# Attention with 32-bit probabilities and values in one product per block, and heads folded by 32-bit products

## The reference

```python
qkv = (xf @ qkv_w.T).reshape(B, H, W, 3, h, d)        # 16 heads of 8 channels
for a in range(KSZ):                                   # 7 x 7 neighbours
    for c in range(KSZ):
        l = einsum('bhijd,bhijd->bhij', q, kac) + bias
        logits.append(l)
attn = softmax(stack(logits), axis=-1)
out = sum over the 49 neighbours t of attn[..., t, None] * vac
y = out @ proj_w.T + proj_b
```

## Time and profile before

| what | value |
|---|---|
| median of 3 runs | 3155.05 us (3146.11 to 3156.77) |
| profiled execution | 3149.2 us |
| its span, first to last instruction | 3147.4 us |
| mean granted TensorE clock | 0.904 of full speed |
| PE busy | 2482.8 us, 79% of the span |
| PEld busy | 2108.7 us, 67% |
| DVE busy | 2353.8 us, 75% |
| ACT busy | 2122.5 us, 67% |
| POOL busy | 2360.1 us, 75% |

### The profile page before, as it was taken

The page is one execution under the profiler, slowest core; times in us unless marked ns, Lnnn a source line. Parts: engine busy times, 40 slices in busy tenths (PEclk is TensorE's granted clock), DMA queues, the critical chain, the costliest instruction groups (busy, mean ns, idle before and its releaser), DMA issues. The chain is left out here.

```text
span 3147.4 us, 119476 instructions
## 1 busy us (share of the span) xinstructions
PE 2482.8 (79%) x34587; PEld 2108.7 (67%) x34692; DVE 2353.8 (75%) x12579; ACT 2122.5 (67%) x5724; POOL 2360.1 (75%) x2808
## 2 busy tenths in 40 slices
PE   4788887888788878888888878888709999999633
PEld 2677777777777777777777777777606666666522
DVE  2688887888788878888788878888746666666444
ACT  0677777777677777777777777777726777777400
POOL 2578888888888888888888888888946777777600
PEclk9999999999899999999999989999959999999855
DMA  2566555555555655555565555556455444444499
GB/s 49 145 126 119 121 124 119 114 122 118 112 106 122 123 118 110 118 117 117 114 120 118 118 109 119 121 117 123 92 99 94 93 92 93 93 93 92 98 314 299
DMA packets 743654, 378.47 MB, mean 120 GB/s; under 512 B 414595, under 2 KB 712227, under 8 KB 743078
## 3 DMA queue, kind: packets, MB, share of 16 engines
q1 hardware_dynamic: 690278, 235.46, 39.5%
q10 hardware_dynamic: 24192, 81.67, 9.9%
q0 software_dynamic: 28608, 54.48, 5.7%
HBM read 232.92 MB, written 98.11 MB: 105 GB/s over the span
## 5 line engine op out<-in xcount | busy, mean ns | idle before, releaser
L1004 ACT ACTIVATE pr<-sc,nmx 128x100 f32<-128x100 f32 x3136 | 922.3, 369 | 103.8 <-DVE nmx L670 100.6
L905 POOL TENSOR_TENSOR pl<-pt 100x512 f16<-100x512 f32 x784 | 815.3, 1040 | 217.9 <-ACT pt L1012 217.4
L670 DVE CUSTOM_DVE_ANT_0 sc<-bank,near 128x100 f32<-128x100 f32 x3136 | 632.3, 256 | 182.7 <-PE bank L490 133.4
L1012 ACT ACTIVATE pt<-bank 100x512 f32<-100x512 f32 x784 | 462.5, 590 | 365.9 <-PE bank L516 353.0
L490 PE MATMUL bank<-kimg,qexp 128*128 (+2 forms) x9408 | 651.5, 221 | 55.3 <-issue 40.0
L490 PEld LDWEIGHTS bank<-kimg,qexp 128*128 128x128 bf16 (+1 forms) x9408 | 567.7, 102 | 103.1 <-issue 71.7
L1385 POOL DMA_INDIRECT yrows<-ye,meta x420 | 451.1, 1074 | 188.6 <-issue 127.6
L516 PE MATMUL bank<-vwin,pt 100*128 100x65 bf16 (+1 forms) x6272 | 417.0, 199 | 202.7 <-DVE om L700 142.6
L516 PEld LDWEIGHTS bank<-vwin,pt 100*128 100x128 bf16 x6272 | 371.9, 102 | 277.1 <-issue 184.6
L911 POOL TENSOR_TENSOR oml<-om 128x256 f16<-128x256 f32 x784 | 483.4, 617 | 57.3 <-DVE om L700 35.4
L499 PE MATMUL bank<-cst_sb,pr 128*100 128x128 f32 x3136 | 503.9, 286 | 0.0
(11 more groups left out here) (150 smaller groups left out, 4665.4 us busy)
## 6 DMA issues: line engine op xcount, KB each, us to landing
vwin<-v_pix SPq DMA_DIRECT2D x1120, 60.5 KB
near<-bias_rows ACTq DMA_DIRECT2D x112, 600.0 KB
y<-yrows SPq DMA_DIRECT2D x112, 224.0 KB, 4.8
qexp<-qring SPq DMA_DIRECT2D x896, 14.0 KB
v_pix<-vrow SPq DMA_DIRECT2D x56, 225.8 KB
xin<-in_x SPq DMA_DIRECT2D x56, 224.0 KB
xres<-in_x SPq DMA_DIRECT2D x112, 112.0 KB, 4.6
x<-xres SPq DMA_DIRECT2D x112, 112.0 KB
```

The source lines that it names most:

```text
L670: i = v.tensor_tensor_reduce(out=sc[:, ring(m, par), k, :], in0=ps_s[m % 2][:, k, :], in1=near[:, st, ct, k, :], scale=-1.0, scalar=-MASKE ...
L905: g.tensor_tensor(pl[:, m % 2], pt[:, m % 2], pt_h[:, m % 2], ALU.subtract).then_inc(s["t_out"], 1)
L1004: i = a.activation(pr[:, r, k, :], sc[:, r, k, :], ACT.Exp, bias=nmx[:, r, k:k + 1], scale=-1.0)
L1012: i = a.activation(pt[:, m % 2].rearrange("p a q -> p (a q)"), ps_t[m % 2][0:NKEY, :], ACT.Copy)
```

## The change

The probabilities pt and the values (vrow, v_pix, vwin) are held as 32-bit numbers only. `weigh` makes one 32-bit product for each block in place of three 16-bit ones and waits for ACT's copy (th_done) in place of POOL's split. `fold_heads` makes one 32-bit product for each tile in place of two 16-bit ones. POOL's `split_t` and `split_l` and DVE's `a_v_l` go, with the tiles pl, oml and fold_b and the semaphores t_out, oml_done and v_h. The lags shrink by one step: weigh from 5 to 4, pick from 6 to 5, the fold from 8 to 7. A row of v_pix has as many bytes as before. The diff, cut to its core:

```diff
-L_T, L_V, L_P, L_H, L_F = 3, 5, 6, 7, 8
+L_T, L_V, L_P, L_F = 3, 4, 5, 7
...
-        v_pix = nc.dram_tensor("v_pix", (B * IMG, 2, VW), BF16, kind="Internal").ap()
+        v_pix = nc.dram_tensor("v_pix", (B * IMG, VW), FP32, kind="Internal").ap()
...
-        vwin = asb("vwin", [NKEY, 2, NTILE, 2, VW], BF16)
+        vwin = asb("vwin", [NKEY, 2, NTILE, VW])
...
                 def weigh(J, m, par):
...
-                    pe.wait_ge(s["t_out"], n + 1)
+                    pe.wait_ge(s["th_done"], n + 1)
...
-                            p_h, p_l = pt_h[:, m % 2, 2 * t + blk, :], pl[:, m % 2, 2 * t + blk, :]
-                            v_h, v_l = (vwin[:, st, 2 * u + t, part, 64 * blk:64 * blk + 65].bitcast(dt)
-                                        for part, dt in enumerate((BF16, FP16)))
-                            for n, (a_, b_) in enumerate(((p_h, v_h), (p_h, v_l), (p_l, v_h))):
-                                mm = pe.matmul(ps_av[m % 2][:, 2 * t + blk, :], a_, b_, start=n == 0, stop=n == 2)
+                            mm = pe.matmul(ps_av[m % 2][:, 2 * t + blk, :], pt[:, m % 2, 2 * t + blk, :],
+                                           vwin[:, st, 2 * u + t, 64 * blk:64 * blk + 65], start=True, stop=True)
                     mm.then_inc(s["av_done"], 1)
 
                 def fold_heads(J, st):
 
-                    pe.wait_ge(s["oml_done"], UPP * J + UNITS * (st + 1))
+                    pe.wait_ge(s["om_done"], UPP * J + UNITS * (st + 1))
...
                     for t in range(NTILE):
-                        for n, part in enumerate((om_h, oml)):
-                            mm = pe.matmul(ps_o[:, t * NQ:(t + 1) * NQ],
-                                           part[:, st, t // 2, 2 * (t % 2):2 * (t % 2) + 2, :].rearrange("p b c -> p (b c)"),
-                                           fold_b[:], start=n == 0, stop=n == 1)
+                        mm = pe.matmul(ps_o[:, t * NQ:(t + 1) * NQ],
+                                       om[:, st, t // 2, 2 * (t % 2):2 * (t % 2) + 2, :].rearrange("p b c -> p (b c)"),
+                                       fold, start=True, stop=True)
                     mm.then_inc(s["o_done"], 1)
...
-                def a_v_l(I):
...
-                LATE_STEPS = {9: a_q_l, 10: a_k_l, 12: a_v_l}
+                LATE_STEPS = {9: a_q_l, 10: a_k_l}
...
-                def split_t(J, m, par):
-
-                    n = UPP * J + m
-                    g.wait_ge(s["th_done"], n + 1)
-                    g.tensor_tensor(pl[:, m % 2], pt[:, m % 2], pt_h[:, m % 2], ALU.subtract).then_inc(s["t_out"], 1)
-
-                def split_l(J, m, par):
-                    n = UPP * J + m
-                    st, u = divmod(m, UNITS)
-                    g.wait_ge(s["om_done"], n + 1)
-                    g.tensor_tensor(oml[:, st, u], om[:, st, u], om_h[:, st, u], ALU.subtract).then_inc(s["oml_done"], 1)
...
-                        i = a.activation(vrow[:, :, 0, 65 * blk:65 * blk + 64],
+                        i = a.activation(vrow[:, :, 65 * blk:65 * blk + 64],
...
-                    i.then_inc(s["v_h"], 1)
+                    i.then_inc(s["v_out"], 1)
```

More of the change, by code:

```diff
@@ L159, in build @@
         pad = asb("pad", [HEADS, PADW, PADW])
-        vrow = asb("vrow", [HALF, NROW, 2, VW], BF16)
+        vrow = asb("vrow", [HALF, NROW, VW])
         sc = asb("sc", [128, RING, 4, NKEY])
@@ L164, in build @@
         pt = asb("pt", [NKEY, 2, 4, 128])
-        pl = asb("pl", [NKEY, 2, 4, 128], FP16)
         rec = asb("rec", [128, 4])
         orec = asb("orec", [128, 4, 8])
-        fold_b = asb("fold_b", [128, NQ], BF16)
-        oml = asb("oml", [128, 2, UNITS, 4, 64], FP16)
         om = asb("om", [128, 2, UNITS, 4, 64])
@@ L204, in build @@
         rowsb = rows[:].bitcast(BF16)
-        pt_h = pt[:].bitcast(BF16)[:, :, :, 1::2]
-        om_h = om[:].bitcast(BF16)[:, :, :, :, 1::2]
         rowsi = rows[:].bitcast(I32)
@@ L218, in build @@
         names = """w_in w_scaled w1_in cst_in rpb_in pad_out gath_in turned win_in bias_done zeroed pad_zero
-            x_in mean_done xc_done sq_done v_h sub_done th_done oml_done
+            x_in mean_done xc_done sq_done sub_done th_done
             var_done ve_done root_done spread_done xn_done q_done q_h q_out k_done k_h k_out v_done v_out v_store q_exp0 q_exp1
-            v_in0 v_in1 s_done max_done exp_done t_done t_out av_done rec_done orec_done om_done
+            v_in0 v_in1 s_done max_done exp_done t_done av_done rec_done orec_done om_done
             o_done o_out proj_done proj_out bias_out near_in0 near_in1 xres_in0 xres_in1 x1_store0 x1_store1
@@ L312, in store_v @@
                     sp.wait_ge(s["v_out"], I + 1)
-                    dst = bass.AP(v_pix.tensor, I * (PAIR * 2 * VW), [[2 * VW, HALF], [HALF * 2 * VW, NROW], [1, 2 * VW]])
-                    sp.dma_start(dst, vrow[:].rearrange("p n a c -> p n (a c)")).then_inc(s["v_store"], 16)
+                    dst = bass.AP(v_pix.tensor, I * (PAIR * VW), [[VW, HALF], [HALF * VW, NROW], [1, VW]])
+                    sp.dma_start(dst, vrow[:]).then_inc(s["v_store"], 16)
                 def spread_q(J, par):
@@ L332, in windows @@
                         sp.wait_ge(s["av_done"], UPP * J - UPP + UNITS * (st + 1))
-                    at = ((J // NPAIR) * IMG + krow(J, st) * W) * (2 * VW)
+                    at = ((J // NPAIR) * IMG + krow(J, st) * W) * VW
                     for kr in range(KW):
-                        src = bass.AP(v_pix.tensor, at + (kr * W + 1) * (2 * VW), [[2 * VW, KW], [TS * 2 * VW, NTILE - 2], [1, 2 * VW]])
-                        sp.dma_start(vwin[kr * KW:(kr + 1) * KW, st, 1:NTILE - 1].rearrange("p t a c -> p t (a c)"), src).then_inc(s[f"v_in{st}"], 16)
+                        src = bass.AP(v_pix.tensor, at + (kr * W + 1) * VW, [[VW, KW], [TS * VW, NTILE - 2], [1, VW]])
+                        sp.dma_start(vwin[kr * KW:(kr + 1) * KW, st, 1:NTILE - 1], src).then_inc(s[f"v_in{st}"], 16)
                     for t, c0 in ((0, 0), (NTILE - 1, W - KW)):
-                        src = bass.AP(v_pix.tensor, at + c0 * (2 * VW), [[W * 2 * VW, KW], [2 * VW, KW], [1, 2 * VW]])
-                        sp.dma_start(vwin[:, st, t].rearrange("p a c -> p (a c)"), src).then_inc(s[f"v_in{st}"], 16)
+                        src = bass.AP(v_pix.tensor, at + c0 * VW, [[W * VW, KW], [VW, KW], [1, VW]])
+                        sp.dma_start(vwin[:, st, t], src).then_inc(s[f"v_in{st}"], 16)
                 def load_res(J, st):
@@ L604, in _ @@
                 v.memset(qexp[:, 1].rearrange("p s t h q -> p (s t h q)"), 0.0).then_inc(s["zeroed"], 1)
-                v.memset(vrow[:, :, 1, 64:65], 0.0)
-                v.memset(vrow[:, :, 0, 64:65], 1.0).then_inc(s["pad_zero"], 1)
+                v.memset(vrow[:, :, 64:65], 1.0).then_inc(s["pad_zero"], 1)
                 v.memset(ones_b[:], 1.0)
@@ L610, in _ @@
                 v.wait_ge(s["cst_in"], 16)
-                v.tensor_copy(fold_b[:], fold)
                 for i in range(2):
@@ L917, in body @@
                                 subtract(J, m, par)
-                            for d, step in ((L_H, split_l), (L_T, split_t)):
-                                if reached(J, m, d):
-                                    step(*back(J, m, par, d))
                         if I is not None and m == A_ROOT:
@@ L930, in _ @@
                 pairs(g, body)
[L931 to L934, removed]
                 for Q in range(PAIRS - 3, PAIRS):
```

## The result

The changed kernel takes 3683.66 us (median of four runs, 3674.18 to 3699.02) where the kernel before takes 3155.91: the ratio is 1.168 (95% interval 1.163 to 1.173). The forecast was 3750, in a range of 3360 to 4000. The profiled execution took 3674.18 us with a span of 3672.4. Of the runs further down, one of the four of the wide fold took 8429.32 us and is left out of its ratio.

What follows compares the result with a forecast made beforehand. The ring's latency, with PE its largest member, bounded the kernel at 39.47 us a pair; PE's 41.7, 7.8 for the clock and 0.7 idle make 50.2, 600 us more over 56 pairs: about 3750 us, range 3360 to 4000.

Steps and rivals of the forecast that it cites:

- PE becomes the bound: Attention, per pair: 32-bit loads add 7.3 us in weigh and 4.8 in folds, PE 41.7 at full clock.
- a sign of a wrong forecast: PE's weight loads: the forecast is wrong if 32-bit loads follow each other faster than 0.11 us.
- The clock: PE after each fold: half clock until the next long 32-bit products, two units between, 7.8 us a pair.
- Idle time: PE in attention: waits for om and q mostly covered, only 0.7 us a pair kept at the loop's ends.
- The new wait for ACT's copy: Weigh, one step nearer its transposes: taken as 0, with 2.8 us a pair (157 us) left to the range.
- POOL: Splits gone: 23.2 us of POOL a pair, with waits of 2.1 us a pair; remaining 10.5 bounds nothing.
- rival D: Weigh and fold: products cost what their columns cost, the ring gets shorter, 36.8 us a pair, 3000 us; chance 0.06.
- the ring: Attention's wait loop: transpose, ACT's copy, POOL's split, weigh, DVE's pick, POOL's split, fold; PE idle 6.7 us a pair.
- Its point of decision: Rival D decides once one 32-bit product of 128 weight columns is under about 0.165 us.

Runs made afterwards that it cites:

- the wide fold: Changed kernel, but each fold product moves 64 columns of constants in place of 16: 3318.17 us, ratio 1.048.
- the two runs that keep the clock up: Changed kernel with 64-column fold products, 3318.17 us; changed kernel with each fold's 14 products spread over several steps, 3301.24 us.
- the ring kernel: Changed kernel, but weigh makes three and fold two 16-bit products, all from high halves, without POOL's splits: 2914.91 us, ratio 0.923.
- all three kernels: Kernel before, 3155.91 us; changed kernel with high-half 16-bit products, no splits, 2914.91; the latter with POOL's subtractions back, unread and unwaited, 3067.89.

## Why the prediction was right, step by step

*PE becomes the bound.* Right, and nearly to the number. The forecast for PE at full clock, with the loop's ends, was 42.4 us a pair; the two runs that keep the clock up take 42.24 and 42.04. The load of a 32-bit product was put at 0.111 us; weigh measured 0.84 us for 0.89 and the fold 3.10 for 3.11. Weigh's loads thus came every 0.105 us, a shade under the 0.11 that was named as a sign of a wrong forecast; it is 0.7 us a pair. That 64 columns take the same 3.10 us as 16 shows the cause: the loads.

*The clock.* The direction was right, the place half wrong, and the size near in part by luck. The step said that it falls with each fold and comes back with the next long 32-bit products, 7.8 us a pair. It cost 6.25. In the pair shown, and in most of the 56, one fold of two is followed by the low level, and there it lasts through three units (1214.02, 1217.43 and 1223.45, the last one partly) in place of two. So there were half as many falls, each of them dearer (6.25 us for 3.9), and the two errors offset each other. Two low stretches of before were little ground for "each", and one was read too short: the one at 1181.40 had begun before its fold, at the loop's end.

```profile
1173.40:1177.40 4.00, 0.00 (x0) 0.00 (x0) 1.41 (x12) 1.55 (x5) 2.48 (x4) 0.50 0.79 103
...
1177.41 1.27 PE L490 MATMUL bank<-kimg,qexp 128*128 x12 [4.34 <-issue]
```

PE stood idle for 4.34 us there, the clock was at half, and the fold came at 1180.66. Why the fold at 1190.81 keeps its clock and the one at 1210.35 does not is not settled: ahead of the second stand the router's logits, eight loads with 8 columns each, which I did not weigh in; no run here moved them. With the old weigh both folds bring the clock down (46 and 51 of 56), so the fold by itself does not decide.

*Idle time.* 0.7 us a pair was kept, 1.09 came. The new wait for ACT's copy was put at 0 with 2.8 for the range: the loads of line 507 wait 41.2 us in all for it, under 1 us a pair.

*POOL.* Its busy time in a pair fell from 33.7 to 11.3, by two thirds, as said. That its removal gives at most the waits for it was wrong: rival D priced the ring at 2.7 us a pair, and it measured 4.35. The term that was too small is DVE. The forecast said that DVE loses two small subtractions and else stays; it fell from 33.1 to 29.8 us a pair, and the two subtractions were 0.74 of that. The mean of gapr (4 columns in 1788 ns) could have been seen in the table by line, where it stands out against its neighbours of 150 to 200 ns.

*Rival D* was still rightly given little: the ring's gain is real, but a 32-bit product costs its loads. Its point of decision also stood on the wrong side of one half of the change: weigh alone at 32 bits, with products of 0.21 us (0.84 / 4), is faster than before, since the ring gives back more than D allowed and PE had 6.7 us of idle time to fill.

*The sum of the parts.* From before to weigh alone a pair goes from 39.47 to 38.04 (-1.43), the fold's loads bring it to 42.24 (+4.20), the low clock to 48.49 (+6.25). Weigh alone is 83 us faster and the fold alone 269 us slower than before; both together are 528 slower, not 186. The idle time of PE is there to be filled once: weigh's 6.6 us of loads (14 x 0.47) take most of it, and from there on each load and each low stretch counts nearly in full. What pays in weigh seems to be the split taken away, and not the product: the ring kernel, with 16-bit products and without POOL's split of om, takes 35.12 us where weigh alone takes 38.04.

## What to carry to other kernels

Before splits are dropped for 32-bit products, count weight loads, not columns: here a 32-bit product of up to 65 columns and 128 weight columns cost 0.21 to 0.22 us, some seven to nine times a 16-bit one (0.025 to 0.031). That paid where three products became one and PE had idle time (weigh). It did not where two became one (the fold), not even alone, with idle time left on PE: 44.44 us a pair in place of 39.47, at a clock of 0.85. And a long run of narrow products can cost the clock of what comes after it, so give them columns or break the run up: each brought 10% back here.

## What the runs showed of the hardware

The granted clock fell to half while PE was busy without a break (the stretches from 1210.4 to 1225.3 above), after a run of 28 products of 16 columns; with 64 columns in the same time the clock of the stretch was 0.99. Such a run did not always do it: in the changed kernel the first strip's fold was followed by a fall in 6 of 56 pairs, the second's in 52. The Trainium skill (TensorE: Matmul & The Clock Gate, Why this matters for your kernels) asks for a TensorE that is kept busy and for no idle gaps; in this trace that was not enough.

A DVE cast of 8 columns took 2649 ns in the mean beside POOL's subtractions and 172 without them, and ended behind the fourth of them in a row. The Trainium skill (GPSIMD Engine Reference, Key points) says that POOL shares its way into SBUF with VectorE and contends with instructions of two SBUF inputs or in a two-port mode. The trace agrees in kind: the pick (line 700 of before), with one of its two inputs in PSUM, kept its 285 to 286 ns in all three kernels. The page gives no size; here a pair grew by 3.13 us, from 35.12.
